# A graph network's segment softmax: one of two inputs of every long VectorE instruction moved to PSUM

## What is computed

```python
# passes 1 and 2: graph attention with 4 heads (between them relu, behind them x + out and a layer norm)
xw = (x @ W).reshape(n, H, D)
logits = leaky_relu(a_src[src] + a_dst[dst], 0.2)             # [E, 4]
ex = exp(logits - segment_max(logits, dst)[dst])
out = segment_sum(xw[src] * (ex / segment_sum(ex, dst)[dst])[..., None], dst).mean(axis=1) + bias
# pass 3: attention for each feature
ef = concatenate([features[src], features[dst]])
att = relu(ef @ W_lin.T + b_lin)                              # [E, 128]
ex = exp(att - segment_max(att, dst)[dst])
new = segment_sum(ex / segment_sum(ex, dst)[dst] * ef, dst)
out = layernorm(x + new @ W_out.T + b_out)
```

## Time and profile before

| | us |
|---|---|
| median of 3 runs | 6597.44 (6593.43 to 6617.95) |
| the profiled execution, its own time | 6601.97 |
| its span, first to last instruction | 6600.1 |

### The profile page before, as it was taken

How to read it: one execution, slowest core, us unless ns; L and a number is a source line. 1 busy time by engine, 2 the same in 40 slices (tenths; PEclk the granted TensorE clock), 3 DMA queues, 4 the chain that set the end, 5 groups by cost and what they waited for, 6 DMA issues and landing times. The chain is left out here.

```text
span 6600.1 us, 94118 instructions
## 1 busy us (share of the span) xinstructions
PE 5032.8 (76%) x26936; PEld 4780.3 (72%) x26936; DVE 3538.8 (54%) x7545; ACT 2745.3 (42%) x4755; POOL 4939.2 (75%) x4707
## 2 busy tenths in 40 slices
PE   2888888888888688888888888577777777777776
PEld 2777777777777677777777777577777777777776
DVE  3344443343334444444444444477777777777777
ACT  1233333333332355555555555344444444444444
POOL 4677777777776777777777777577777777777775
PEclk6666666666666666666666666655555555555555
DMA  6222222222222222222222222222322233223222
GB/s 137 54 61 61 61 62 62 61 59 62 62 62 51 60 66 63 63 65 64 63 65 64 63 65 65 59 82 81 85 82 81 81 85 81 81 81 84 83 81 57
DMA packets 377187, 462.43 MB, mean 70 GB/s; under 512 B 148438, under 2 KB 256511, under 8 KB 376634
## 3 DMA queue, kind: packets, MB, share of 16 engines
q0 software_dynamic: 150336, 218.46, 15.2%
q1 hardware_dynamic: 219606, 242.02, 12.6%
q10 hardware_dynamic: 7156, 0.89, 0.1%
HBM read 425.44 MB, written 39.55 MB: 70 GB/s over the span
## 5 line engine op out<-in xcount | busy, mean ns | idle before, releaser
L962 POOL DMA_INDIRECT rows<-tab,idx_now x4696 | 4935.8, 1051 | 1606.4 <-issue 1428.8
L1653 PE MATMUL bank_t<-own,hot_t 112*128 112x8 f32 x6288 | 1283.2, 345 | 722.0 <-ACT hot_t L1453 681.3
L1653 PEld LDWEIGHTS bank_t<-own,hot_t 112*128 112x128 f32 x6288 | 1259.7, 309 | 757.2 <-ACT hot_t L1453 477.4
L1686 PE MATMUL bank_s<-share,rows 128*65 128x52 f32 (+7 forms) x6288 | 1093.0, 359 | 0.4 <-DVE share L1225 0.4
L1225 DVE TENSOR_TENSOR share<-hot,prob 128x400 f32<-128x400 f32 (+2 forms) x786 | 497.6, 688 | 1091.4 <-ACT prob L1525 1087.4
L1686 PEld LDWEIGHTS bank_s<-share,rows 128*65 128x65 f32 x6288 | 1016.6, 210 | 5.0 <-DVE share L1225 0.6
L1742 PE MATMUL bank_e<-own,hot_t 112*128 112x64 f32 x3144 | 689.7, 418 | 1.9 <-issue 1.9
L1742 PEld LDWEIGHTS bank_e<-own,hot_t 112*128 112x128 f32 x3144 | 685.0, 332 | 2.0 <-issue 2.0
L1774 PE MATMUL bank_s<-hot,prob 128*128 128x112 f32 x3144 | 672.5, 408 | 0.0
L1774 PEld LDWEIGHTS bank_s<-hot,prob 128*128 128x128 f32 x3144 | 653.0, 319 | 0.0
L1451 ACT ACTIVATE away<-rel_t,minus_row 112x1536 f32<-112x1536 bf16 x393 | 616.8, 1570 | 60.8 <-DMA rel_t<-rel_row 54.4
(11 more groups left out here) (220 smaller groups left out, 6205.6 us busy)
## 6 DMA issues: line engine op xcount, KB each, us to landing
rel_t<-rel_row SPq DMA_DIRECT2D x262, 336.0 KB
rows<-tab,idx_now POOLq DMA_INDIRECT x4696
rel_t<-rel_runs SPq DMA_DIRECT2D x131, 336.0 KB
cut<-cut_row SPq DMA_DIRECT2D x524, 60.0 KB
own<-tab SPq DMA_DIRECT2D x262, 63.0 KB
tab<-row SPq DMA_DIRECT2D x131, 112.0 KB
tab<-row SPq DMA_DIRECT2D x131, 63.0 KB
own<-tab SPq DMA_DIRECT2D x131, 56.0 KB
```

The costliest lines, as they stand in the source:

```text
L962: nc.gpsimd.indirect_dma_start(rows_of[p][:, G * c.s + j, :], None, halves[p], bass.IndirectOffsetOnAxis(ap=idx_now[:, c.s, j:j + 1], axis ...
L1653: nc.tensor.matmul(added[:, j, :, :], hot_t[k][:, P * j:P * j + P], own[c.s][:, 0:H].unsqueeze(1).to_broadcast([W, 2, H]), start=j == 0, s ...
L1686: done = nc.tensor.matmul(summed[:, :, LO[j]:HI[j]], rows_g[:, at + j, 0:D + 1], share[:, j, :, 0:SUBS[j]], start=not opened, stop=j == G ...
```

## The change

1. Long two-input instructions of DVE get one of their inputs in PSUM. `upto` and the column numbers `col_no` lie in PSUM, also `prob` of stages 1 and 2; in stage 3 the scans run on `ps_t` in PSUM, the first one in place, and ACT writes relu and exponential to `middle` in PSUM. The PSUM banks are dealt out anew.
2. In stage 3 `ps_t` is a single buffer in PSUM. The large transposition of a unit therefore moves from two units ahead (`turn_theirs`) to just ahead of the unit's scans (`last_most`). Two small transpositions of the outer chunks (`turn_ends`) take its old place, for the halos.
3. In stage 3 ACT takes the exponential twice, into `middle` for DVE and into `prob3` for PE.
4. `col_no3` shares a bank with the sums of PE, so `one_hots3` of a unit waits until the sums of the unit before are done.
5. The permutation into `rel_runs` leaves ACT's queue. SP issues it in 131 parts, one for each unit of stage 2.

```diff
-        bank_t = ps("bank_t", [P, 1024])
-        bank_e = ps("bank_e", [P, 1536])
...
+        psum = ps("psum", [P, 4096])
+        bank_t, bank_e, bank_s = psum[:, 0:1024], psum[:, 1024:2560], psum[:, 2560:3072]
+        bank_h, bank_c = psum[:, 3072:3584], psum[:, 3584:4096]
+        upto = bank_e[0:G * H, 0:SPAN]
+        col_no = bank_e[:, 256:256 + W]
+        prob = [bank_e[:, 512 * k:512 * k + G * H].rearrange("p (j h) -> p j h", h=H) for k in (1, 2)]
...
+        ps_t = psum[:, 0:2 * LONG]
+        added3 = psum[:, 1024:1024 + G * D].rearrange("p (j c) -> p j c", c=D)
+        extra3 = psum[0:W, 1024 + G * D:1024 + G * D + D]
+        middle = psum[:, 2048:2048 + G * D].rearrange("p (j c) -> p j c", c=D)
...
+        summed3 = bank_c[:, 0:W]
+        col_no3 = bank_c[:, 256:256 + W]
...
+                    if p == 1:
+                        run = rel_row[bass.ds(UE * c.u, 1)].offset
+                        sp.dma_start(bass.AP(rel_runs.tensor, run, [[P, G], [QUAD, RUNS], [1, QUAD]]),
+                                     bass.AP(rel_row.tensor, run, [[QUAD, G], [RUN, RUNS], [1, QUAD]]))\
+                            .then_inc(rel_spread, 16)
...
             def one_hots3(c):
 
+                if not c.below(1):
+                    dve.wait_ge(sums_ready, 2 * NU + c.u)
...
-            def turn_theirs(c):
...
+            def turn_ends(c):
+
+
                 dve.wait_ge(rows_in[c.s], landed(2, c, G - 1, LASTC - 1, LASTG - 1))
                 dve.wait_ge(first_in[c.s], landed(2, c, 1, 1))
-                nc.vector.transpose(ps_t[c.s % 3][:, :, HALO:HALO + RUN].rearrange("p j (c b) -> p c j b", b=QUAD),
+                for k in range(2):
+                    at = G * c.s + (G - 2) * k
+                    nc.vector.transpose(outer[c.s % 3][:, :, 2 * QUAD * k:2 * QUAD * k + 2 * QUAD]
+                                        .rearrange("p j (c b) -> p c j b", b=QUAD),
+                                        rows_e[:, at:at + 2, D:2 * D].rearrange("p c (j a) -> p c j a", a=QUAD))\
+                        .then_inc(ends_turned, 1)
+
+            def last_most(c):
+
+                at = G * c.s
+                dve.wait_ge(beside_kept, c.u + 1)
+                nc.vector.transpose(ps_t.rearrange("p (j e) -> p j e", j=2)[:, :, HALO:HALO + RUN]
...
+                dve.wait_ge(body_turned, c.u + 1)
+                segment_most(2, 2 * NU + c.u, c, P, cut3[c.k], ps_t, ps_t, 2 * LONG, HALO)
...
-                nc.vector.scalar_tensor_tensor(out=logit3[:, :, :], in0=near[:, :, :], scalar=0.0, in1=over[:, :, :],
+                nc.vector.scalar_tensor_tensor(out=logit3[:, :, :], in0=near[:, :, :], scalar=0.0, in1=middle,
...
-                if p == 0:
-                    act.wait_ge(rel_out, 32)
-                    for i in range(RUNS):
-                        act.dma_start(bass.AP(rel_runs.tensor, QUAD * i, [[UE, NU], [P, G], [1, QUAD]]),
...
-                nc.scalar.activation(prob3[k][:, :, D:2 * D], logit3[:, :, :], ACT.Exp).then_inc(prob_ready, 1)
+                nc.scalar.activation(middle, logit3[:, :, :], ACT.Exp).then_inc(prob_ready, 1)
+                nc.scalar.activation(prob3[k][:, :, D:2 * D], logit3[:, :, :], ACT.Exp).then_inc(prob_kept, 1)
```

More of the change, by code:

```diff
@@ L270, in build @@
         hot3 = [sb_late(f"hot3{k}", [P, G, W]) for k in range(2)]
-        ps_t = [sb_late(f"ps_t{k}", [P, 2, LONG]) for k in range(3)]
+        outer = [sb_late(f"outer{k}", [P, 2, 4 * QUAD]) for k in range(3)]
         back = sb_late("back", [P, G, D])
@@ L327, in build @@
         extra = bank_c[0:W, 0:3 * D]
-        beside = bank_t[:, 0:4 * HALO].rearrange("p (s j w) -> p s j w", s=2, j=2)
+        beside = bank_h[:, 0:4 * HALO].rearrange("p (s j w) -> p s j w", s=2, j=2)
         banks.close()
@@ L1323, in last_stats @@
                 dve.wait_ge(out_made, m + 1)
-                nc.vector.tensor_tensor(mix[:, :], extra[:, 0:D], own3[c.s][:, D:2 * D], ALU.add).then_inc(pre_ready, 1)
+                nc.vector.tensor_tensor(mix[:, :], extra3, own3[c.s][:, D:2 * D], ALU.add).then_inc(pre_ready, 1)
                 dve.wait_ge(pre_ready, m + 1)
@@ L1362, in with_own @@
                 dve.wait_ge(own3_ready, c.u + 1)
+                if not c.below(2):
+                    dve.wait_ge(out_made, c.u - 1)
                 dve.wait_ge(back_ready, c.u + 1)
@@ L1368, in _ @@
             p = 2
+            dve.wait_ge(row_kept_a, 2 * NU)
+            nc.vector.tensor_copy(col_no3, col_f[:, :]).then_inc(test_step, 1)
+            dve.wait_ge(test_step, 28)
             one_hots3(unit(0))
-            turn_theirs(unit(0))
-            turn_theirs(unit(1))
+            turn_ends(unit(0))
+            turn_ends(unit(1))
             last_most(unit(0))
@@ L1385, in _ @@
                 at = G * c.s
[L1386 removed]
+                nc.vector.tensor_tensor(prob3[k][:, :, 0:D], middle, rows_e[:, at:at + G, 0:D], ALU.mult)\
                     .then_inc(share_ready, 4)
@@ L1524, in _ @@
                     act.wait_ge(logit_ready, n + 1)
-                    nc.scalar.activation(prob[c.k][:, :, :], logit[:, :].rearrange("p (j h) -> p j h", h=H), ACT.Exp)\
+                    nc.scalar.activation(prob[c.k], logit[:, :].rearrange("p (j h) -> p j h", h=H), ACT.Exp)\
                         .then_inc(prob_ready, 1)
@@ L1550, in relu_over @@
                 act.wait_ge(added_ready, 2 * NU + c.u + 1)
-                nc.scalar.activation(over[:, :, :], over[:, :, :], ACT.Relu).then_inc(over_ready, 1)
+                nc.scalar.activation(middle, over[:, :, :], ACT.Relu).then_inc(over_ready, 1)
             p = 2
@@ L1740, in own_part3 @@
                     pe.wait_ge(near_ready, c.u)
+                if not c.below(3):
+                    pe.wait_ge(pre_ready, c.u - 2)
                 for j in range(G):
@@ L1746, in beside_runs, with begins, stops @@
             def beside_runs(c):
-                def ends(d, at):
-                    return ps_t[c.plus(d).s % 3][:, :, at:at + HALO]
+                def begins(d):
+                    return outer[c.plus(d).s % 3][:, :, 0:HALO]
+                def stops(d):
+                    return outer[c.plus(d).s % 3][:, :, 4 * QUAD - HALO:4 * QUAD]
                 alone = c.at_least(NU - 1)
-                pe.wait_ge(ps_turned, c.u + (1 if alone else 2))
+                pe.wait_ge(ends_turned, 2 * c.u + (2 if alone else 4))
                 if not c.below(1):
                     pe.wait_ge(beside_kept, c.u)
-                nc.tensor.matmul(beside[:, 0, :, :], up, ends(0, RUN), start=True, stop=c.below(1))
+                nc.tensor.matmul(beside[:, 0, :, :], up, stops(0), start=True, stop=c.below(1))
                 if not c.below(1):
-                    nc.tensor.matmul(beside[:, 0, :, :], up_around, ends(-1, RUN), start=False, stop=True)
-                done = nc.tensor.matmul(beside[:, 1, :, :], down, ends(0, HALO), start=True, stop=alone)
+                    nc.tensor.matmul(beside[:, 0, :, :], up_around, stops(-1), start=False, stop=True)
+                done = nc.tensor.matmul(beside[:, 1, :, :], down, begins(0), start=True, stop=alone)
                 if not alone:
-                    done = nc.tensor.matmul(beside[:, 1, :, :], down_around, ends(1, HALO), start=False, stop=True)
+                    done = nc.tensor.matmul(beside[:, 1, :, :], down_around, begins(1), start=False, stop=True)
                 done.then_inc(beside_ready, 1)
@@ L1780, in last_mix @@
                 pe.wait_ge(mean_ready, m + 1)
-                nc.tensor.matmul(extra[:, 0:D], mean[:, :], w_last[:, :], start=True, stop=True).then_inc(out_made, 1)
+                nc.tensor.matmul(extra3, mean[:, :], w_last[:, :], start=True, stop=True).then_inc(out_made, 1)
             beside_runs(unit(0))
```

46 lines of the change are left out of this document (19 added, 27 removed).

## The result

The changed kernel takes 6352.74 us (median of 4 runs, 6348.44 to 6356.89) against 6598.86 of the kernel before, run beside it: a ratio of 0.9622, 95% interval 0.9602 to 0.9642. The forecast was 6327, so the time lies 26 us above it and inside the range. The profiled execution took 6352.61, its span is 6350.8 us.

A forecast was written before the change was run, and what follows sets the result against it. POOL's gathers, held up by DVE's second SBUF read, were taken as the bound but for early stage 1. 6602 - 76 - 44 - 151 = 6331 us profiled, 6327 as median; range 6230 to 6475.

The forecast's parts named there:

- Rival 1: All stages: the locks stay or something else lengthens the gathers, only POOL's 40 us of waiting go; 6557, 4%.
- The start and stage 1: 76 forecast: PE's halo matmul 53 us earlier without ACT's four DMA issues, plus 23 us from 15.02 us a unit throughout stage 1.
- Stage 2: 44 forecast: Stage 2's unit falls from 15.44 to 15.1 us: 0.34 x 130 = 44 us.
- PE and ACT's 15.02: Stage 1: what PE and ACT need by themselves, 15.02 us a unit, seen early while POOL is ahead.
- POOL's floor: Twelve undisturbed gathers a unit, 12 x (0.94 + 0.305) = 14.95 us.
- Stage 3: 151 forecast: Stage 3's round falls from 17.86 to 16.7 us: 1.16 x 130 = 151 us.
- part of these 9% comes back: Stage 3: PE's lines, 5.27 against 4.81 us in stage 1, get faster as PE pauses less; A down to 15.8 at most.
- A: Stage 3's circle of waits through PE, from logit to PE's sums and `hot`, closed by `hot`'s new wait: 17.01 us.
- B: Stage 3's circle of waits through ACT: relu, exponentials, large transposition, scans, `back`, `over`, next relu: 16.33 us.
- the allowance of 4.5 us: Whole kernel: the median lies 4.5 us below the profiled execution, taking 6331 to 6327.
- Rivals 3 and 4: Stage 3: PSUM operands dear in part, 6410 to 6600, 14%; DVE with PSUM on both sides at half pace, 6952, 6%.
- Rival 2: All stages reach POOL's floor, all 500 us and the 40 go: 6057, anything up to 6230; 6%.

The follow-up runs named there:

- Experiment 7: Changed kernel with stage 3's single `ps_t` back in SBUF, orders and waits unchanged: 6367.19 us, ratio 0.9645.
- experiment 9: Changed kernel with stage 3's column numbers read from SBUF again and `hot`'s wait for PE's sums removed: 6269.02 us, ratio 0.9497.
- experiment 10: Changed kernel, stage 3's column numbers in SBUF, no `hot` wait for PE's sums, ACT's one-hots ahead of the relu: 6219.4 us, ratio 0.9424.
- 6: Changed kernel with `upto`, `col_no` and `prob` of stages 1 and 2 back in SBUF: 6431.54 us, ratio 0.9740.
- Experiment 5: Changed kernel with the permutation into `rel_runs` back on ACT's queue at the start of stage 1: 6406.62 us, ratio 0.9702.
- experiment 2: Changed kernel with stage 3's column numbers in another PSUM bank, so `hot` no longer waits for PE's sums: 6272.24 us, ratio 0.9514.
- experiment 4: Changed kernel with column numbers in another PSUM bank, `hot` free of PE's sums, and ACT's one-hots ahead of the relu: 6111.84 us, ratio 0.9271.

## Why the prediction was right, and where it missed

**The bound, and what removes it: right.** The gathers beside DVE's long instructions were held by the second SBUF read: in stage 3 of the changed kernel not one of 1570 gathers takes over 1 us. Experiment 7 put the scans' tile back, 9 and 10 the input of `hot`, 6 the three inputs of stages 1 and 2, and each got long gathers back. `hot` is the cleanest case, since nothing but an input moved. Rival 1 (the locks stay) is out. The exponential in PSUM for the multiplication of stage 3, with the second exponential that pays for it, was never put back alone, so its worth isn't known. The Trainium skill, page "SBUF — State Buffer", section "Who interferes with whom", says that a DVE instruction with two SBUF inputs contends with GpSimd instructions that read SBUF; the traces agree. The same section reports that `tensor_tensor` did not stall a DMA; for these indirect DMAs experiment 10 shows the opposite, 1.94 us instead of 0.94.

**The start and stage 1: 76 forecast, 78.5 measured.** Experiment 5 gives the start alone 54 (forecast 53); the halo matmul stands at 112.15 instead of 162.94, though the stage's first line began 2.6 us later. SP's 131 parts show no cost: experiment 5 takes them away, and stage 2, where they are issued, lasts 2010.1 us instead of 2010.2.

**Stage 2: 44 forecast, 48 measured**, at 15.07 us a round for the 15.1 taken. In stage 1, gathers (14.98 us a unit over units 5 to 125) and the spreading line (14.99) keep one pace, so "PE and ACT's 15.02" and POOL's floor can't be told apart there. In stage 2 they can: gathers take 14.98 a unit and the line 15.08, and its distance from a unit's first gather grows from 14.5 us (unit 5) to 25.6 (unit 120). POOL is no longer the bound of stage 2, as the prediction had it.

**Stage 3: 151 forecast, 122.5 measured. This is the miss**, and the step that failed is "part of these 9% comes back". Both circles were summed rightly: A 17.01 against 16.97 in the round shown and 16.93 over 110 units; B 16.33 against 16.24, once A was open (experiment 2). The round I took, 16.7, was A with a part of PE's clock back. Nothing came back: the granted clock of the stage went from 0.58 to 0.55, and the lines of PE in A took 5.28, 0.58 and 5.43 us where they had taken 5.27, 0.58 and 5.44. The error is the condition: PE paused less, as forecast, but it still stands still once in each round, 3.46 us ahead of line 1784 (5.24 before), and its groups took as long as ever. The comparison of the two lines was sound: line 1653 with its 8 columns took 5.26 us behind a long pause too, so the 4.81 of stage 1 is a mean of such groups and shorter ones (4.50 at 303.43 in the trace of before). Taking A as summed, 17.01, the term is 0.85 x 130 = 110 us and the forecast 6367; at the measured 16.93 it is 121 us and 6357.

**The rest of the 26 us.** By spans the forecast saving was 271 and the measured one 249.3: 21.7 us, of which stage 3 holds 28.5 and the other terms -6.8; that these took a part of the miss back is luck. The remaining 4 is the allowance of 4.5 us between the profiled execution and the median, which after is nothing (6352.61 against 6352.74).

**What would show it.** The period of stage 3 was to be near 16.7 and is 16.93. Five signs came as named: gathers at 945 ns, no long ACT issue, 14.99 in stage 1 to its end, `hot` waiting 2.05 us for PE, DVE no longer waiting for rows. One was wrong: POOL does not wait for DVE's `share` but, 219.6 us in 101 waits, for ACT's `idx_now`, the indices that ACT copies behind the halo copy. It shows the same thing, that POOL is ahead by its whole ring, but by another hand.

**The price of PSUM operands: next to nothing.** The scans take 2.16 and 2.05 us (2.16 and 2.06 in the earlier trace rows), the first with input and output in PSUM; `hot` 1.55 (1.56); logit 0.94 (0.95). By the means of their groups the dearest are the large transposition, which now writes to PSUM, with 993 ns instead of 978, and the first scan of stages 1 and 2 with 620 instead of 607. Rivals 3 and 4 are out. The Trainium skill's page "VectorE: DVE Perf Modes", section on the errata, gives a PSUM input 62 cycles more; no instruction here shows them.

**Rival 2, POOL's floor everywhere**, is what experiment 4 reached, at 6112. It was no consequence of the change, since two waits stood between: `hot` on the sums, and the exponential behind ACT's one-hots.

## What to carry to other kernels

When a resource conflict is removed, sum every circle of waits through the other engines, start to start, before paying out the gain; two nearly equal circles (16.97 and 16.24 here) must be opened together, and one alone can be worth nothing. Ask of each moved operand whether its engine is the bound there: the same lock cost 14 us under a circle of 16.9 and 245 us at POOL's floor, and a tile moved to save it cost 84 us through the wait that came with it. Take durations at the clock that the rows show, and don't count on a better one because the round shortens: with a pause of 3.46 us left in each round, none came here (in experiment 4, at 14.98 us a round and 334.0/130 = 2.6 us of pause, a little did).

## What the runs showed of the hardware

- An indirect DMA's issue on GpSimd (0.94 us, and 0.30 to the next) that starts while DVE reads two SBUF inputs ends 0.74 to 0.75 us behind a scan and 0.82 us behind `hot`, up to 1.2 us late here (experiment 9); DVE's own instruction keeps its length (2.16 and 2.06 us in experiment 7). With one input in PSUM the gather is not touched. The other way round nothing was held up: in stage 3 of experiment 7 a gather was already running when the first scan began in 127 of 131 units, and these gathers took 0.94 to 0.95 us and the scans 2.16.
- ACT is a little faster when it writes to PSUM: relu 0.81 us instead of 0.84, and 0.80 against 0.83 for the two exponentials of the same input; the means over 131 of each are 815 against 843 ns and 797 against 827. The Trainium skill, page "ScalarE: Activation LUTs", section "Step-by-step: what each stage is for", says that ACT writes to PSUM faster than to SBUF, and the rows agree.
- The granted clock of stage 3 fell while PE's busy share of it rose: 0.58 and 74% at 17.86 us a round, 0.55 and 79% at 16.93, and 0.58 again with 81% at 16.24. The spreading line's groups took 5.27 and 5.28 us in the first two, and 538.03/100 = 5.38 in the third, where they wait for one-hots in between. At nearly the same round (16.9 to 17.1 us, over 4500 to 5700 us) the changed kernel shows 0.56, experiment 5 0.54 and experiment 7 0.58, with 5.27 us a round on that line in each. So the mean clock of a stage did not tell the speed of a given group here.
